# Projecting the second attention's keys inside the first attention, and storing them unmasked

## The reference

```python
x = x + xattn0(layernorm(x), ctx)   # 16 heads of 8
x = x + ffn0(layernorm(x))          # 16 experts, top 4 of 16, width 128
x = x + xattn1(layernorm(x), ctx)   # 16 heads of 64
x = x + ffn1(layernorm(x))          # 8 experts, top 1, width 512

def xattn1(x, context):             # per batch
    q = (x @ Wq).reshape(B, Nq, 16, 64).transpose(0, 2, 1, 3)
    k = (context @ Wk).reshape(B, Nk, 16, 64).transpose(0, 2, 1, 3)
    v = (context @ Wv).reshape(B, Nk, 16, 64).transpose(0, 2, 1, 3)
    attn = softmax(q @ k.T / 8)
    return (attn @ v) reshaped to (B, Nq, 1024) @ Wo + bo
```

## Time and profile before

| what | us |
|---|---|
| median of 3 runs | 386.0 (385.28 to 392.62) |
| the profiled execution | 391.18 |
| its span | 389.5 |
| PE busy | 325.4 (84%) |
| DVE busy | 216.1 (55%) |
| ACT busy | 156.9 (40%) |
| POOL busy | 144.6 (37%) |
| attention 0 with what leads to it | 0 to 76.3 |
| drain and tables | 76.3 to 107 |
| expert loop 0 | 107 to 178 |
| attention 1 | 197 to 311 |
| expert loop 1 | 311 to 369 |

### The profile page before, as it was taken

The page is one execution under the profiler, slowest core; times in us unless marked ns, Lnnn a source line. Parts: engine busy times, 40 slices in busy tenths (PEclk is TensorE's granted clock), DMA queues, the critical chain, the costliest instruction groups (busy, mean ns, idle before and its releaser), DMA issues.

```text
span 389.5 us, 8873 instructions
## 1 busy us (share of the span) xinstructions
PE 325.4 (84%) x2867; PEld 264.1 (68%) x2878; DVE 216.1 (55%) x695; ACT 156.9 (40%) x379; POOL 144.6 (37%) x225
## 2 busy tenths in 40 slices
PE   7779999968959889799977999999999847978820
PEld 3457677645448778675357899999999744967710
DVE  7433776653239778781435858786756352434421
ACT  5533533546746454543634454535444200112110
POOL 6031277677453334303764013633111032111052
PEclk9979999986569999998998999999999966899975
DMA  7999511111277898732111001100000008587322
GB/s 181 332 289 281 165 37 37 43 35 35 81 201 208 221 264 227 212 91 71 45 46 24 5 2 29 35 15 22 9 8 8 2 20 261 179 267 236 127 64 58
DMA packets 45780, 43.55 MB, mean 112 GB/s; under 512 B 4312, under 2 KB 40784, under 8 KB 45744
## 3 DMA queue, kind: packets, MB, share of 16 engines
q1 hardware_dynamic: 29360, 27.31, 24.5%
q0 software_dynamic: 4096, 9.18, 8.4%
q10 hardware_dynamic: 12288, 6.60, 5.7%
HBM read 26.16 MB, written 16.91 MB: 111 GB/s over the span
## 4 chain that ended last, share of the span: by engine, by line
PE 57%; DMA 12%; issue 10%; POOL 8%; DVE 6%; ACT 2%; POOLq 2%; SPq 2%; ACTq 0%
DMA shared<-wp_dram 5%; PE bank_S L1738 5%; PE bank_S L1470 5%; PE bank_M L1556 4%; PE bank_S L1771 4%; DMA xin<-dispatched 4%; PE bank_M L1519 4%; PE bank_O L1493 3%; PE bank_T L1479 3%; PE bank_M L1493 3%; POOL dispatched L627 3%; PE bank_S L1410 2%; PE bank_O L1448 2%; PE bank_O L1454 2%; PE bank_S L1424 2%
## 5 line engine op out<-in xcount | busy, mean ns | idle before, releaser
L1738 PE MATMUL bank_S<-xeT,shared 128*128 128x256 f32 (+1 forms) x256 | 54.7, 350 | 5.9 <-DMA shared<-wp_dram 5.8
L635 POOL DMA_INDIRECT G<-expert_out,yslot x40 | 38.6, 966 | 29.9 <-DMA expert_out<-yo 18.3
L1738 PEld LDWEIGHTS bank_S<-xeT,shared 128*128 128x128 f32 x256 | 40.1, 204 | 10.1 <-issue 5.8
L627 POOL DMA_INDIRECT dispatched<-XN,slot_u x40 | 40.0, 1000 | 14.0 <-issue 9.8
L515 POOL DMA_DIRECT2D xin<-dispatched x36 | 23.7, 657 | 51.9 <-PE bank_T L1726 28.9
L1294 DVE TENSOR_SCALAR scratch<-bank_S,shared 128x128 f32<-128x128 f32 x64 | 18.0, 345 | 27.3 <-PE bank_S L1738 27.3
L598 POOL TENSOR_SCALAR var_eps<-mv 128x1 f32<-128x1 f32 (+1 forms) x18 | 4.2, 231 | 74.7 <-DVE mv L977 74.6
L1726 PE MATMUL bank_T<-C,xin 128*128 128x128 f32 x80 | 18.2, 295 | 13.8 <-DMA xin<-dispatched 13.6
L719 ACT ACTIVATE PT<-bank_T 77x512 f32<-77x512 f32 x40 | 22.9, 589 | 14.9 <-PE bank_T L1479 14.9
L908 ACT ACTIVATE xeT<-bank_T 128x256 f32<-128x256 f32 (+1 forms) x48 | 16.6, 346 | 29.4 <-PE bank_T L1726 18.5
L1312 DVE TENSOR_SCALAR scratch<-bank_S,shared 128x256 f32<-128x256 f32 x32 | 15.5, 483 | 16.0 <-PE bank_S L1738 15.9
(11 more groups left out here) (234 smaller groups left out, 776.9 us busy)
## 6 DMA issues: line engine op xcount, KB each, us to landing
shared<-wp_dram SPq DMA_DIRECT2D x16, 514.0 KB, 4.7
dispatched<-zeros SPq DMA_DIRECT2D x8, 1024.0 KB, 9.8
shared<-wp_dram SPq DMA_DIRECT2D x32, 193.0 KB, 3.2
expert_out<-yo ACTq DMA_DIRECT2D x16, 256.0 KB, 3.9
xin<-dispatched POOLq DMA_DIRECT2D x24, 128.0 KB, 3.9
xin<-dispatched SPq DMA_DIRECT2D x8, 128.0 KB, 3.6
expert_out<-yo ACTq DMA_DIRECT2D x8, 128.0 KB, 4.4
xin<-dispatched POOLq DMA_DIRECT2D x12, 64.0 KB, 4.0
```

The lines of the kernel that those rows point to most:

```text
L627: nc.gpsimd.indirect_dma_start(out=xs_dram, out_offset=bass.IndirectOffsetOnAxis(ap=slot_u[:, b, k:k + 1], axis=0), in_=XN[:, b, :], in_of ...
L635: nc.gpsimd.indirect_dma_start(out=G[:, b % 2, k, :] if layer == 0 else G[:, b // 4, b % 4, :], out_offset=None, in_=ys_dram[layer], in_of ...
L1738: ins = nc.tensor.matmul(bank[hbk][:, 128 * unit * c:128 * unit * (c + 1)], wbuf[:, q, 128 * c:128 * c + 128], xeT[:, u0:u0 + unit, :], st ...
```

## The change

- K1 and the keys and queries of attention 0 get memory of their own. K1 loses its second version: one array of 8 x 616 columns, where a pair of heads fills 128 partitions, 64 each. All writes of zeros go, and with them their semaphores.
- The 16 projections move into slots 1 to 5 of attention 0: two ahead of the second score call, into S2 and S3 (slots 1 to 5), two behind the sums, into T0 and T1 (slots 1 to 3). ScalarE copies each in one instruction of 128 partitions. Wk is loaded ahead of SP's zero stores.
- The two dummy products of a slot stay in slots 6 and 7 only.
- On VectorE `choose` moves from the slot after the logits to the end of the same slot, behind `values_0`; the inversion of the sums goes ahead of the logits eviction; rank, place and scatter come one slot earlier, and there are 11 slots instead of 12.
- Dummy products are added in the drain: 5 behind proj in each of slots 8 to 10, 8 ahead of the transpose in slot 9, and 3 ahead of each of three waits in `tables(0)`.
- Scores in attention 1: 16 products of 77 columns with 64 contraction rows, the halves of the partitions in turn, each pair into two different banks. Since S(g) now gets the four heads of one half, the values and Wo are taken in another order of heads (`head_at`).
- PE's order in a batch of attention 1: scores 2 and scores 3 become one call behind pv 2 and the logits. VectorE's order there stays.

```diff
@@ PE, attention_0
+def k1_in_slot(i, half):
+    first = (None, 0, 4, 8, 12, 14)[i] if i < 6 else None
+    if first is None or half and i > 3:
+        return []
+    return [(first + k, KEYS_T[k]) for k in (2 * half, 2 * half + 1)]
...
-                for i in range(B + 4):
+                for i in range(B + 3):
...
-                    if 0 <= i - 4:
-                        rank(0, i - 4)
-                    if 0 <= i - 1 < B:
+                    if 0 <= i - 3:
+                        rank(0, i - 3)
+                    if i == B + 1:
+                        keep_clock(bank["T0"], DRAIN_WARM[1])
+                    k1(i, 0)
+                    if 6 <= i < B:
                         use("O", J("O", "u", 0, i - 1, 0))
                         keep_clock(bank["O"], SLOT_WARM)
...
                     if 0 <= i - 1 < B:
                         sums_0(i - 1)
+                    k1(i, 1)
...
-                    if i >= B:
-                        k1(*K1_DRAIN[i - B])
                     if 0 <= i - 1 < B:
                         proj(0, i - 1)
+                    if i >= B:
+                        pe.wait_ge(freed["T0"], J("T0", "keysT", B - 1, 2))
+                        keep_clock(bank["T0"], DRAIN_WARM[0])
@@ VectorE, attention_0
-                    if 0 <= i - 3 < B:
-                        choose(0, i - 3)
+                    if 0 <= i - 1 < B:
+                        sums_0(i - 1)
                     if 0 <= i - 2 < B:
                         logits_out(0, i - 2)
                     if 0 <= i - 1 < B:
                         values_0(i - 1)
+                    if 0 <= i - 2 < B:
+                        choose(0, i - 2)
@@ ScalarE, attention_0
                     if 0 <= i - 2 < B:
                         xn_scaled(i - 2)
+                    k1_out(i, 0)
+                    if 0 <= i - 2 < B:
                         xnT_out(0, i - 2)
+                    k1_out(i, 1)
@@ POOL, drain
-                if i == B + 2:
-                    pool.wait_ge(rt_rstd, B)
-                    nc.gpsimd.memset(K1[64:128, 0:4, 0, :], 0.0).then_inc(keys1_zeroed, 1)
-                if 0 <= i - 4:
-                    scatter(0, i - 4)
-            pool.wait_ge(keys1_zeroed, 3)
+                if 0 <= i - 3:
+                    scatter(0, i - 3)
@@ PE, attention_1
                 for g in groups:
-                    o = use(f"S{g}", J(f"S{g}", "scores", 1, b, g))
-                    for c in (2 * g, 2 * g + 1):
-                        ins = nc.tensor.matmul(o[:, 2 * M * (c % 2):2 * M * (c % 2 + 1)], QT1[:, b % 2, c, :],
-                                               K1[:, c, :, M * b:M * b + M], start=True, stop=True)
-                    ins.then_inc(filled[f"S{g}"], 1)
+                    use(f"S{g}", J(f"S{g}", "scores", 1, b, g))
+                for g0 in range(groups[0], groups[-1], 2):
+                    for j in range(GH):
+                        for k in range(2):
+                            r = slice(64 * k, 64 * k + 64)
+                            ins = nc.tensor.matmul(bank[f"S{g0 + k}"][:, M * j:M * j + M],
+                                                   QT1[r, b % 2, 2 * g0 + j, :], K1[r, 2 * g0 + j, M * b:M * b + M],
+                                                   start=True, stop=True)
+                            if j == GH - 1:
+                                ins.then_inc(filled[f"S{g0 + k}"], 1)
...
-                    scores(b + 1, (2,))
                     pv(b, 2)
                     if routed:
                         logits(1, b - 2)
-                    scores(b + 1, (3,))
+                    scores(b + 1, (2, 3))
                     pv(b, 3)
@@ PE, tables(0): ahead of the waits for mexp, act_bc and ohj
+                if layer == 0:
+                    keep_clock(bank["T0"], DRAIN_WARM[2])
...
-                    k1(10, 1)
+                    keep_clock(bank["T0"], DRAIN_WARM[2])
...
-                    k1(11, 1)
+                    keep_clock(bank["T0"], DRAIN_WARM[2])
```

96 lines of the change are left out of this document (39 added, 57 removed).

## The result

The changed kernel takes 428.09 us (423.54 to 428.64), the kernel before beside it 387.75 us (385.28 to 392.62): ratio 1.1033, interval 1.093 to 1.114. That is slower, as forecast, but by 40 us instead of 11.5, and outside the range of 387 to 405.

The account below looks back on a forecast made before the run. TensorE's program was taken to set attention 1's pace, with VectorE holding pv 3 and POOL the path before the loop. Terms -1.8 + 9.65 + 3.6 = +11.45 us gave 397.5 on the median; range 387 to 405.

Parts of the forecast that it names:

- The clock term: Attention 1: two of the five new holes make the granted clock fall, 1.8 us each: +3.6 us, bounds 0 and +9.
- The stall: Attention 1: pv 3 waits for bank O behind VectorE's shift, pv_out and logits eviction: +1.67 us in each of five batches, 8.35.
- The small terms of the first two batches: Attention 1: batch 1, proj(0) waits for bank M, +0.75 us; batch 0, the late norm holds xT, +0.3.
- the first rival: Stall without a fallen clock, TensorE being full on both sides of each hole: 393.9 us, chance 0.22.
- The call: Attention 1: a two-group score call of four pairs takes 0.87 us, plus 0.15 for entering and leaving the tiled form.
- The start of the loop: Ahead of the expert loop: keys in the slots +6.1 us, shorter drain -7.9, net -1.8, bounds -5.3 and +0.6.
- the keys: Attention 0: key projections moved into slots 1 to 5 cost +6.1 us, bounds +2.6 and +8.5.
- The last scatter: Drain of attention 0: one slot less ends it at 95.8 instead of 103.66, -7.9 us, before the slots' +6.1.
- Series loads: Rival for attention 1's score calls: weight loads follow each other, 16 calls at +0.85 us each: 411 us, chance 0.08.
- row tiling at its full factor: Rival for attention 1's score calls: 16 calls, each 0.36 us less: 392 us, chance 0.07.
- The slots did not swallow the keys: Denies the attention 0 rival that keys cost 2.6 us instead of 6.1, with one clock fall less: 392, chance 0.06.
- the stall came: Denies the attention 1 rival that pv 3 isn't held by bank O and scores save 2.1 us: 382 us, chance 0.08.

Follow-up runs that it names:

- VectorE's order: Changed kernel with pv_out 2 and choose ahead of shift(b+1, 2) on VectorE: 411.89 us, 1.060 to the kernel before; again on a slower chip 466.71 us, 1.080.
- moved calls with the old products: Kernel before with both later score calls behind pv 2 and the logits, old 154-column products, VectorE in the order without a hole: 395.79 us, ratio 1.010.
- narrow pairs: Kernel before with 64-row, 77-column pair products, both later calls behind pv 2 and the logits, VectorE's order without the hole: 456.75, 454.95, 457.73 us (1.064, 1.056, 1.074).
- jobs 2 to 4: Three groups of kernels, each run on one chip beside the kernel before, which itself took 431.35, 429.34 and 426.00 us there.
- job 1: Four kernels run on one chip beside the kernel before (388.74 us), three of them variants of the changed kernel: 402.45, 411.89 and 418.67 us.
- first half alone: Slots, drain and memory as changed, attention 1 with the old product shape and orders on unmasked keys, against the kernel before: 439.42 and 436.56 us (1.024, 1.011).
- twice the columns: Changed kernel in VectorE's order with 154 columns instead of 77 in each pair product, the second 77 unread: 455.88 and 456.65 us (1.063, 1.061).
- filling products: Narrow pairs on the kernel before, plus four bf16 products of 204 columns ahead of each pair call: 448.01 us, 1.056 to the kernel before.
- full rows: As the narrow pairs on the kernel before, but each 77-column product takes all 128 rows on the masked keys: 456.75 us, 1.074 to the kernel before.

## Why the prediction was wrong

**The clock term failed**: 3.6 us was forecast and about 27 came. It said that two of five holes would make the clock fall, at 1.8 us each. Both parts were wrong. The trigger: the clock fell within the pair call, ahead of the hole (265.6), and without any hole (VectorE's order, three falls with 17.0 us cold; moved calls with the old products, five with 34.1; the last falls of the narrow pairs in jobs 2 to 4). A hole adds to it (11 to 15 us with the old products). The number and size: nine falls in attention 1 instead of the one of before and two new ones, 3.4 to 10.2 us long (the last goes on behind the stage), 56 us in all, at a cost of half. "PE is full on both sides of each hole", which made me take few falls, took busy time for work. All 13.49 busy microseconds of a batch were treated as alike, and nothing asked what the change does to the work within them.

**The stall** was right in its mechanism: five times, released by VectorE's lg, TensorE idle for 1.69 us each where 1.85 was forecast. In the one batch that can be read at the full clock pv 3 comes 2.1 us later (10.87 against 8.73 from q), forecast 1.67, so the term was low by some 2 us over five batches. The small terms of the first two batches came too: a wait of 0.59 us ahead of proj (forecast 0.75), and the wait for XA grew from 0.69 to 1.93 (forecast 0.3). Without a fallen clock the result would have been the first rival, some 3 us over its 393.9 (an estimate from these rows).

**The call**: 1.05 us start to start with its switch, forecast 0.87 + 0.15 = 1.02. Right. The reading behind it, that a weight load sets the pace and loads of the two halves overlap, fits the three forms of the call. What I did not see is that the call of before has half as many passes.

**The start of the loop**: -1.8 us was forecast for all that lies ahead of attention 1, and the first q starts 1.8 earlier (195.4 against 197.2). But that is luck: 6.1 - 7.9 was forecast and +1.5 + 4.9 - 5.3 - 2.8 measured (the table of stages). The first scores came 1.5 us later, behind a cold stretch at 9.6 to 13.0; kernels with the old first half show both starts, 13.9 to 14.1 and 15.4 to 15.7, so this is no effect of the change. The slots grew by 4.9 us instead of 6.1, although a stretch of 6.8 us at half speed went away (3.4 us); at one clock the keys cost about 8.3, the upper bound. The last scatter ended 1.1 us later instead of 1.8 earlier: the last batch of the drain ran cold, scatter 6 started at 94.37 where 85.8 + 6.1 = 91.9 was forecast, and scatter 7 waited for its rows for 0.80. Loop 0 then took 2.8 us less, which I had not forecast and have not explained. In three other executions of the same first half (job 1) attention 0 took 67.9, 67.9 and 74.0 us instead of 62.3, where that of before took 57.3 to 57.4 in four, and the first q started at 197.2, 198.7 and 205.6, where with the old first half it started at 195.2 beside them. The first half measured alone, on the slower chips, is a loss of 5 to 10 us. That slots without their dummies are the reason stays open.

**The rivals.** Series loads (411 us) had the wrong mechanism, and row tiling at its full factor (392) too, and with it the "up to 2x" of the Trainium skill ("TensorEngine Tiling (Array Packing)", Theoretical Speedup): here the halves do run side by side, 1.05 against 1.80 us, yet against the products they replaced that is worth 9%. The slots did not swallow the keys, and the stall came. None of the rivals had a clock that fails in each batch; the upper bound of the clock term, +9, was the place where it should have stood.

**The 40 us**, as far as the runs split them, by the kernels on chips where the kernel before takes 386 to 391 us: the moved calls 4 (1.010), the pair form with the first half 19 (VectorE's order against the moved calls without a hole, 1.060 less 1.010), the hole 17 (changed kernel against VectorE's order, 1.103 less 1.060). The 1.060 has no interval, its four executions lie between 407.6 and 417.2. How the 19 divide is not shown: the first half alone cost 5 to 10 and the pairs with the moved calls 24 to 32 (1.056 to 1.074) on the slower chips, where ScalarE's holes are part of both.

**Open.** What quantity the clock follows. Moved calls, narrow pairs and idle time each go with more time at half speed; with twice the columns, with all rows or with filling products the narrow pairs' falls without a hole are gone. That the rows in use do nothing is not shown, as full rows were measured only among ScalarE's holes. Why ScalarE copies late on some chips, and longer in some kernels than in others, is not known. Whether the pairs would lose as much on an undisturbed chip was not measured alone, only with the first half (1.060). No version here beats the kernel before.

## What to carry to other kernels

A TensorE program that is busy all the time at the full clock may hold that clock by its densest products. Before replacing wide products, even ones that multiply zeros, by narrow ones with the same result, count passes (weight loads) for the time, and for the clock ask which dense product is left between the thin ones. And cost a fall of the clock by the cold stretches the trace already shows (3.4 to 10.2 us in the kernel before, its end left out), not by the length of the hole that may start it. When a run is meant to have no hole, list the engine's waits in its trace before reading the clock: on the slower chips here there were others, elsewhere in the batch.

## What the runs showed of the hardware

- The clock fell from 2.4 to 1.2 GHz with TensorE idle for no more than 0.2 us in the 15 us before (265.6 of the changed kernel), and one program kept or lost it by execution: 390.45 us at a mean granted clock of 0.92, 408.62 at 0.87.
- Holes of 1.6 to 3.2 us ahead of pv 1 were followed by 10.2 or 13.7 us at half speed, all but one (1.60 us, pairs filled).
- Twice the columns in the score calls gave -10 and -12 us by the medians of two jobs, though each such call took 0.2 us longer. With 5.4 us of filling products attention 1 took 148.7 us instead of 153.9 to 155.2.
- Two 64-row products run side by side, loads included: 0.066 us per pass against 0.11 on full rows.
- The same program takes 386 to 391 us on some chips and 426 to 431 on others, with TensorE idle for 0.4 to 2.0 us where the profile names no releaser and for 1.0 to 3.2 us behind a late ScalarE, and falls of the clock behind these.
